# Attention and scan kernel: v projected straight into key rows, a second projection in place of the first chunk's swap, and a new order of the attention steps

## What is computed

```python
def _attn(a, sin, cos, ga, ba, gb, bb, Wq, Wkv, Wo, bo):
    an = _ln(a, ga, ba)
    bn = _ln(a, gb, bb)
    q = an @ Wq
    k, v = jnp.split(bn @ Wkv, 2, axis=-1)
    ...                                # 4 heads of 16 channels
    q = _rope(q, sin, cos)
    k = _rope(k, sin, cos)
    dots = jnp.einsum('bhid,bhjd->bhij', q, k)
    attn = jax.nn.softmax(dots, axis=-1)
    out = jnp.einsum('bhij,bhjd->bhid', attn, v)
    ...
    return jax.nn.elu(out @ Wo + bo)
...
xi = _attn(rows of x, ..._i);  xj = _attn(columns of x, ..._j)
return x + (xi + xj) / 2
```

## Time and profile before

| | us |
|---|---|
| median of 3 runs | 334.65 (333.85 to 337.41) |
| profiled execution | 336.71 |
| its span in the trace | 334.6 |
| TensorE busy | 235.9 (70%) |
| VectorE busy | 203.9 (61%) |
| ScalarE busy | 171.3 (51%) |
| GpSimd busy | 126.9 (38%) |

### The profile page before, as it was taken

One profiled execution on the slowest core, in us unless ns is written; L12 is line 12 of the kernel. 1 busy time (PEld: TensorE's weight loads), 2 busy tenths in 40 slices (PEclk: granted clock), 3 DMA queues, 4 the chain that ended last, 5 costly groups with the idle time before them and its releaser, 6 DMA issues.

```text
span 334.6 us, 7775 instructions
## 1 busy us (share of the span) xinstructions
PE 235.9 (70%) x3138; PEld 142.4 (43%) x3138; DVE 203.9 (61%) x333; ACT 171.3 (51%) x298; POOL 126.9 (38%) x104
## 2 busy tenths in 40 slices
PE   0366776886749694674259669998999867976453
PEld 0143444554425453452248335653444434445312
DVE  2668668684635453347535495899786868285333
ACT  2142554577553737183533674367447644933282
POOL 1411669114615160550040087367496971400000
PEclk9999798999996969597556989999799997997758
DMA  7510010433030303410354300000000000002002
GB/s 191 207 63 33 33 66 32 109 84 82 16 96 0 90 10 64 94 36 0 73 112 91 75 18 0 2 5 3 0 4 2 0 2 2 0 3 65 0 1 63
DMA packets 34243, 15.26 MB, mean 46 GB/s; under 512 B 31008, under 2 KB 31520, under 8 KB 34080
## 3 DMA queue, kind: packets, MB, share of 16 engines
q1 hardware_dynamic: 32480, 13.67, 16.1%
q10 hardware_dynamic: 1728, 1.10, 1.2%
HBM read 5.42 MB, written 2.10 MB: 22 GB/s over the span
## 4 chain that ended last, share of the span: by engine, by line
PE 38%; DVE 22%; ACT 17%; issue 11%; DMA 5%; SPq 5%; POOL 1%; ACTq 1%; DVEq 0%; POOLq 0%
PE ring L565 17%; PE score L565 8%; PE oz L565 4%; DMA rot_swap<-rot_sin 4%; PE ring L570 3%; PE p_turn L565 3%; SPq L537 3%; SPq L524 2%; DVE ln_v L864 2%; PE p_turn L570 2%; DVE mix L1142 2%; DVE ln_s L844 2%; ACT prob_t L1302 2%; DVE xhat L879 2%; DVE rot_sin L1006 2%
## 5 line engine op out<-in xcount | busy, mean ns | idle before, releaser
L1527 POOL TENSOR_TENSOR a_msk<-dt_fin,c_sb 128x512 f32<-128x512 f32 x32 | 39.7, 1239 | 34.4 <-DVE dt_fin L981 22.6
L1302 ACT ACTIVATE prob_t<-p_turn 128x512 f32<-128x512 f32 x32 | 17.7, 595 | 41.9 <-PE p_turn L570 41.8
L565 PE MATMUL score<-k_bd,q_rot 32*64 32x128 f32 x512 | 23.0, 330 | 17.6 <-POOL q_rot L895 16.0
L1142 DVE TENSOR_TENSOR mix<-dec,g_m 128x512 f32<-128x512 f32 x32 | 31.4, 987 | 2.2 <-ACT dec L1384 1.5
L1047 DVE TENSOR_REDUCE s_max<-score 128x16 f32<-128x1024 f32 x16 | 19.5, 1221 | 20.7 <-PE score L565 20.7
L1006 DVE SCALAR_TENSOR_TENSOR rot_cos<-ring,b_att,p_sb 128x512 f32<-128x512 f32 x15 | 11.2, 747 | 30.2 <-PE ring L565 17.2
L570 PE MATMUL ring<-c_sb,xhat 128*128 128x128 f32 x44 | 11.1, 401 | 25.1 <-DVE xhat L879 21.3
L565 PEld LDWEIGHTS score<-k_bd,q_rot 32*64 32x64 f32 x512 | 18.2, 165 | 23.5 <-POOL q_rot L895 18.2
L565 PE MATMUL score<-a_msk,c_sb 128*128 128x512 f32 x44 | 25.2, 656 | 0.0
L895 POOL TENSOR_TENSOR q_rot<-rot_cos,rot_swap 128x512 f32<-128x512 f32 x7 | 8.9, 1266 | 42.3 <-DMA rot_swap<-rot_sin 42.3
L1512 POOL TENSOR_TENSOR dtx<-xv,dt_fin 64x512 f32<-64x512 f32 x16 | 19.8, 1239 | 13.2 <-PE p_turn L565 12.2
(11 more groups left out here) (177 smaller groups left out, 582.6 us busy)
## 6 DMA issues: line engine op xcount, KB each, us to landing
...
```

The costliest lines, as they stand in the source:

```text
L565: return pe.matmul(dst, lhsT, rhs, start=start, stop=stop, skip_group_check=True)
L1142: v.tensor_tensor(mix[:, e % LAPS, :, :], dec[:, e % LAPS, :, :], wide(g_m[:, e // 4 % 2, e % 4, :], SSM_H), ALU.mult)\
L1302: a.activation(prob_t[:, e % 2, 4 * hp:4 * hp + 4, :].rearrange("p k n -> p (k n)"), PT[hp], ACT.Identity)\
L1527: gp.tensor_tensor(a_msk[:, m % LAPS, :, :], deep(dt_fin[:, 0, SSM_H * m:SSM_H * (m + 1)], GRID), wide(cst("tri"), SSM_H), ALU.mult).then_ ...
```

## The change

- **v.** Before, v was projected with channels as rows, drained with its bias by ScalarE (`v_sb`), turned by four transposes (`vt`) and copied to `v_bd` in two instructions. Now the normalised input is the stationary operand and the weight the moving one, so that v comes out with keys as rows: 8 products in the first pass, 32 in the second. ScalarE copies it straight to `v_bd`. The bias of v is folded into the output bias by two products (`bo`, in step 3).
- **Chunk 0.** k and q are projected a second time with swapped columns, onto the outer halves of the banks; the second multiplication of the rotation reads these, and no swap transfer is made. Both masks of k come from ScalarE, `k_rot` from VectorE. k(1) is projected before the first step, onto a `p_turn` bank.
- **Order of steps.** Before: even steps `wo`, `v`, `k` and `yt`, odd steps `vt` and `q`. Now: even steps `q` of the next chunk in slot b, `v` and `yt` in slot c; odd steps `wo` in a and `k` in b. Each q is projected one step later than before, each k one step later too.
- **ScalarE** executes the exponential before the slots a and b.
- **SyncE** issues both swaps of a second-pass chunk before the stores of a turned one.
- The normalising of tiles 1 to 3 is spread otherwise; the weight preparations move from ahead of steps 3 and 5 to the ends of steps 7 and 9, with `fold` in step 8.
- The parameter array grows by 128 columns in the first transfer and by 256 in the second.

```diff
-FOLD_STEP = 4
+FOLD_STEP = 8
+WEIGHTS = (dict(q=0, qs=1, k=2, ks=3, v=4), dict(q=0, k=1, v=2))
+BIASES = (0, 5)
...
-    steps = {-1: ([("xr", 0), ("k", 0), ("q", 0), ("xr", 1), ("v", 0), ("vt", 0)], [], [])}
+    steps = {-1: ([("xr", 0), ("k", 0), ("q", 0), ("v", 0), ("xr", 1), ("k", 1)], [], [])}
     for n in range(ATT_STEPS):
         g, odd = divmod(n, 2)
-        if n == 0:
-            a, b, c = [("k", 1)], [], []
-        elif n == 1:
-            a, b, c = [("xr", 2), ("q", 1)], [("v", 1)], [("k", 2), ("xr", 3)]
+        if n == 1:
+            a, b, c = [], [], [("xr", 2), ("k", 2)]
         elif n == 2:
-            a, b, c = [("vt", 1), ("q", 2)], [("v", 2)], [("k", 3)]
+            a, b, c = [], [("q", 2)], [("v", 1), ("xr", 3)]
+        elif n == 3:
+            a, b, c = [], [("k", 3)], [("bo", 0)]
         elif odd:
-            a, b, c = [("vt", g + 1)], [("q", g + 2)], []
+            a, b, c = [("wo", g - 2)] if g - 2 < ATT_CHUNKS - 1 else [], [("k", g + 2)], []
         else:
-            a, b, c = [("wo", g - 2)], [("v", g + 1)], [("k", g + 2), ("yt", g - 3)]
+            a, b, c = [("wo", g - 2)] if g - 2 == ATT_CHUNKS - 1 else [], [("q", g + 1)], [("v", g), ("yt", g - 3)] if n else []
...
-        if use == ("q", 0):
+        if use in (("q", 0), ("k", 1)):
...
+                sp.wait_ge((k_added, q_ready)[slot], g)
...
-            for g in range(CHUNKS):
+            for g in range(1, CHUNKS):
...
+                swap(CHUNKS + g, 1)
                 sp.wait_ge(y_turned, g + 1)
                 for a in range(2):
                     for m in range(2):
                         sp.dma_start(turned_w[a, m, g],
                                      y_tok[64 * a:64 * a + 64, g, :].rearrange("p (k m c) -> p k m c", k=4, m=2)[:, :, m, :])\
                             .then_inc(turned_out, 16)
-                swap(CHUNKS + g, 1)
...
+                if kind in ("q", "k"):
                     for r in range(2):
                         for a in range(2):
-                            last = mm(half_of(use, r)[64 * a:64 * a + 64, :], w_att[d][64 * r:64 * r + 64, at:at + DIM],
+                            last = mm(half_of(use, r)[64 * a:64 * a + 64, :], weight(w_att[d][64 * r:64 * r + 64, :], d, kind),
                                       xn_cols(d, c, r, a))
+                    if g == 0:
+                        for r in range(2):
+                            for a in range(2):
+                                last = mm(outer_half(use, r)[64 * a:64 * a + 64, :],
+                                          weight(w_att[d][64 * r:64 * r + 64, :], d, kind + "s"), xn_cols(d, c, r, a))
+                elif kind == "v" and d == 0:
+                    for k in range(2):
+                        for a in range(2):
+                            for u in range(2):
+                                last = mm(half_of(use, u)[:, DIM * (2 * k + a):DIM * (2 * k + a) + DIM],
+                                          xn_cols(0, c, u, a)[:, P * k:P * k + P], weight(w_att[d][64 * u:64 * u + 64, :], d, "v"))
+                elif kind == "v":
+                    for u in range(2):
+                        for k in range(2):
+                            for a in range(2):
+                                for m in range(2):
+                                    for r in range(2):
+                                        row = 64 * m + 32 * r
+                                        last = mm(half_of(use, u)[row:row + 32, DIM * (2 * k + a):DIM * (2 * k + a) + DIM],
+                                                  xn_i[64 * r:64 * r + 64, 16 * c + 8 * u + 4 * k + 2 * a + m, :],
+                                                  weight(w_att[d][64 * r:64 * r + 64, :], d, "v"))
...
-                elif kind == "vt":
-                    pe.wait_ge(v_copied, g + 1)
-                    last = turn(dst, v_sb[:, :])
+                elif kind == "bo":
+                    pe.wait_ge(mid_in, 16)
+                    pe.wait_ge(bias_here, 2)
+                    for d in range(2):
+                        at = BIASES[d] + WEIGHTS[d]["v"]
+                        last = mm(dst[:, d:d + 1], par("wo_" + "ji"[d]), b_att[:, at:at + 1])
...
+                    if e == 0:
+                        drained(pe, ("k", 1))
...
-            ln_mean(v, 1)
             ln_vector_b(v, 0)
-            ln_centre(v, 1)
             ln_vector_c(v, 0)
             v.wait_ge(bias_made, 1)
-            v.tensor_copy(b_att[:, 0:3], oz[:, 0:3]).then_inc(bias_here, 1)
+            v.tensor_copy(b_att[:, 0:4], oz[:, 0:4]).then_inc(bias_here, 1)
+            v.wait_ge(xa_in[1], 32)
+            ln_vector_a(v, 1)
+            ln_vector_b(v, 1)
...
+                    if g >= 1:
+                        v.scalar_tensor_tensor(rot_sin[:, slot, :].rearrange("p (t j) -> p t j", j=GRID),
+                                               middle(use).rearrange("p (t j) -> p t j", j=GRID), bias, table_of(d, sin_s[d][:, 0:(GRID, CW)[d]]),
                                                ALU.add, ALU.mult).then_inc(rotated, 1)
+                    else:
+                        v.scalar_tensor_tensor(rot_swap[:, slot, :].rearrange("p (r n) -> p r n", r=2), outer(use),
+                                               bias_at(d, kind + "s"),
+                                               wide(sin_s[0][:, :], 2),
+                                               ALU.add, ALU.mult).then_inc(rotated, 1)
+                elif kind == "bo":
+                    src = filled(v, use)
+                    for d in range(2):
+                        v.tensor_tensor(bo_v[:, d:d + 1], src[:, d:d + 1], col("bo_" + "ji"[d]), ALU.add).then_inc(bo_ready, 1)
...
+                if use == ("k", 0):
+                    k_sum(v, 0)
+                    ln_vector_c(v, 1)
                 if use == ("q", 0):
-                    ln_vector_b(v, 1)
-                    ln_vector_c(v, 1)
-                    v.wait_ge(xa_in[2], 32)
-                    ln_vector_a(v, 2)
-                    k_sum(v, 0)
-                    v.wait_ge(k_added, 1)
-                    k_mask(v, 0, 1)
                     q_sum(v, 0)
-                    v.wait_ge(bias_made, 2)
-                    v.tensor_copy(b_att[:, 3:6], oz[:, 3:6]).then_inc(bias_here, 1)
+            v.wait_ge(bias_made, 2)
+            v.tensor_copy(b_att[:, 4:8], oz[:, 4:8]).then_inc(bias_here, 1)
...
-                if n == FOLD_STEP - 1:
-                    late_weights()
-                if n == FOLD_STEP + 1:
-                    late_scales()
...
-                    ln_vector_b(v, 3)
+                    ln_vector_c(v, 2)
+                    v.wait_ge(xa_in[3], 32)
+                    ln_vector_a(v, 3)
                 for use in att_steps[n]:
                     if use[0] in ("k", "q"):
                         att_use(use)
-                    if use == ("q", 1):
-                        ln_vector_c(v, 3)
                 if n == 0:
+                    v.wait_ge(xa_in[2], 32)
+                    ln_vector_a(v, 2)
                     ln_vector_b(v, 2)
-                    ln_vector_c(v, 2)
-                    v.wait_ge(xa_in[3], 32)
-                    ln_vector_a(v, 3)
+                if n == 2:
+                    ln_vector_b(v, 3)
+                    ln_vector_c(v, 3)
                 g, odd = divmod(n, 2)
-                if odd and 0 <= g - 2 < ATT_CHUNKS:
-                    c = g - 2
+                c = g - 2
+                if (0 <= c < ATT_CHUNKS - 1) if odd else c == ATT_CHUNKS - 1:
                     v.wait_ge(wo_biased, c + 1)
                     v.scalar_tensor_tensor(y_t[:, c // CHUNKS, c % CHUNKS, :], wo_e[:, :], 1.0, wo_b[:, :], ALU.min, ALU.add)\
                         .then_inc(y_ready, 1)
                 for use in att_steps[n]:
                     if use[0] not in ("k", "q"):
                         att_use(use)
+                if n == FOLD_STEP - 1:
+                    late_weights()
+                if n == FOLD_STEP + 1:
+                    late_scales()
...
-                    d = g // CHUNKS
-                    if g >= 1:
-                        filled(a, ("vt", g - 1))
-                    a.wait_ge(bias_here, 1 + d)
-                    a.activation(in_order(d, v_sb[:, :]), as_made(d, middle(use)), ACT.Identity,
-                                 bias=b_att[:, 3 * d + 2:3 * d + 3]).then_inc(v_copied, 1)
-                elif kind == "vt":
-                    src = filled(a, use)
...
-                        a.activation(v_bd[rows, g % 2, :, HD * m:HD * m + HD], src[rows, :].rearrange("p (t d) -> p t d", d=HD),
+                        a.activation(v_bd[rows, g % 2, :, HD * m:HD * m + HD], middle(use)[rows, :].rearrange("p (t d) -> p t d", d=HD),
...
-                    a.activation(k_bd[:, 0, 0, :], k_rot[:, :], ACT.Identity, scale=cst("head_mask")[:, 0:1]).then_inc(k_ready, 1)
-                att_use(use)
+                    for r in range(2):
```

(7 more changed lines are left out.)

109 lines of the change are left out of this document (68 added, 41 removed).

## The result

| | before | after |
|---|---|---|
| median (4 runs each) | 335.07 us | 322.11 us |
| lowest to highest | 333.85 to 337.41 | 317.66 to 322.88 |
| profiled execution, span | 336.71, 334.6 | 321.89, 319.8 |
| ratio of runs, 95% interval | | 0.956 [0.945, 0.968] |

The forecast was 317.5 (310 to 325), with 0.92 for faster. The mechanisms happened as described, and most of the laps came within 1 us.

The account below looks back on a forecast made before the run. Attention was taken as bound by q standing in SyncE's queue behind the stores. -19.8 + 1.3 + 0.9 = -17.6 took the profiled 336.71 to 319.1, 317.0 for runs; 0.5 for small waits gave 317.5 us (310 to 325).

Parts of the forecast that it names:

- Front: Start up to scores 4: first scores at 20.8 us instead of 23.79, scores of step 4 at 49.0 against 56.66.
- the removed transfers cover the second projections: Before the first scores: k and q cost 1.1 us more each, but chunk 0's swap transfers and their waits go.
- Step 4 to 6: From scores 4 to scores 6: a lap of 10.3 us, without a late y_t in step 3.
- Step 7: Step 7's s_cen ends 12.6 us later than step 5's 59.2, at 71.8.
- Step 8: x_tok loads and weight block arrive late together: scores start at 76.3 us, block decides by 0.3, s_max at 77.7.
- 8 to 10: Lap from step 8 to 10: 13.2 us against 15.8, with the fold holding step 9's scores to 86.7.
- The laps from 10: Steps 10 to 14: two laps of 13.0 us plus 1.0 for the scales; scores 14 at 116.6 against 136.35.
- y_t's wait: Odd second-pass steps: y_t waits for ScalarE's drain behind the exponential, from 1.35 to 2.45 us after s_cen's end.
- v behind q's rotation: Second pass: v waits for q's rotation, 7.0 us after odd s_cen's end, takes 1.3; next scores queue behind it.
- q hidden by 0.7 at the least: Second pass: with its swap issued before the stores, q_rot is hidden by at least 0.7 us.
- The rival by which v is dear: Second pass: v's 64 instructions cost far more than 20 ns each; 328 us at 62 ns, 362 at 195; chance 0.04.
- Tail: Scores 14 to x_tok: the 15.7 us of before plus 1.3 for chunk 5's drain; 0.9 more for the second x_tok.

Follow-up runs that it names:

- a_dma0: The changed kernel with chunk 0's swap made by transfers again, without the second projection's eight products: 318.0 us, ratio 0.951.
- a_fold5: The changed kernel with weight block, fold and scales three steps earlier (block behind step 4, fold in step 5): 314.9 us, ratio 0.935.
- a_act: The changed kernel with ScalarE's old order, the output product drained ahead of the exponential of the same odd step: 316.7 us, ratio 0.944.
- a_act_v: The changed kernel with ScalarE's old order (drains ahead of the exponential) and v projected ahead of q's projection: 317.5 us, ratio 0.945.
- b_sp: The kernel before with only SyncE's order changed, both swaps of a second-pass chunk ahead of the four stores: 312.8 us, ratio 0.933.

## Why the prediction was right, and where it was not

- **Front.** Scores 0 at 20.8, measured 21.16; step 2: 36.0, 36.48; step 3: 45.0, 45.59; step 4: 49.0, 50.07. Right within 1.1. v's 8 products (16 instructions) were taken as 1.8 and took 1.97 at the lower level; the biases 1.53 in place of 0.8. The statement that the removed transfers cover the second projections was tested by itself (a_dma0) and holds.
- **Step 4 to 6.** 10.3, measured 11.1. v of the first pass at 1.11 and 1.37, not 0.9.
- **Step 7.** Its s_cen was to end at 71.8 and ends at 74.3: 1.0 of that was there at step 5, and 1.5 came in steps 6 and 7, where the granted clock stood at 0.50 from 68 to 70 us.
- **Step 8.** Scores at 76.3, measured 77.85, released by q_rot; the block was to decide by 0.3, and it does decide, by far more: w_ops starts at 78.27 and s_max at 81.32, in place of 77.7. Of these 3.6, 2.5 are step 7's late s_cen and 0.9 are y_t, which took 1.60 there in place of 0.69.
- **8 to 10 is the step that failed in size**: 13.2 forecast, 16.0 measured, the largest single miss. Scores 8, set by the loads, were only 1.6 late, but s_max behind the block was 3.6 late, so 2.1 more lie between the two than I had. From that s_max to scores 9 it takes 7.7, with 0.88 idle on TensorE for o_t, 1.27 for q's rotation and 1.36 for the drain of y, near my 7.9. The other 0.9 lie behind step 9's s_cen: I had scores 10 start 0.1 after its end, and they start 1.0 after it. And block, fold and scales cost 7 us where they stand, as a_fold5 shows, where my sum had them nearly hidden behind the loads. They did not only lie beside the loads' stall: they held s_max and o_t, and with them the products behind.
- **The laps from 10.** 14.0 and 13.1 for 10 to 12 and 12 to 14, measured 14.4 and 12.7. The two holds in them were named: y_t's wait at 1.05 (measured 0.95 to 1.10, and 1.3 per lap by a_act), and v behind q's rotation (0.9 and 0.4 by the laps of a_act and a_act_v from 10 to 12 and 12 to 14).
- **q hidden by 0.7 at the least**: right, q_rot ends 4.6, 3.6 and 1.5 ahead of the scores of steps 10, 12 and 14 (at 89.2 for scores at 93.84). One row was misread on the way: the transfer at 97.69 stands behind two more issues at 96.36 and ends after q_rot's start at 99.04, so it is the swap of the next k and not q's. The 4.0 from q's first issue to q_rot, which the cover goes by, are right.
- **v's 64 instructions at 1.3**: 1.10, 17 ns each, and once 1.68. The rival by which v is dear is out.
- **Tail.** 17.0 from scores 14 to x_tok, 16.8 measured. Behind x_tok it takes 182.0; I had 183.4, the 182.5 of before and 0.9.

So the sum was 4.4 short at scores 14 (15.35 gained against 19.8), 1.6 of it built up by scores 8 and 2.8 in the lap from 8 to 10. Of the 4.4, 0.2 and 1.4 came back in the tail, so that the profiled execution is 2.8 above the 319.1 of the sum. The 1.4 are luck: the same program behind x_tok differs by 6 from profile to profile. The 4.6 of the medians have another part that no mechanism stands for: I had put the median 2.06 below the profiled time, as before, and for the changed kernel it lies 0.2 above it (2.8 and 2.3, less the 0.5 that I had added for small waits).

What the prediction did not ask, because it only compared the new order with the old, is how much of the gain the new order of steps is the reason for. It listed y_t's wait and v's place as costs, and had it summed a lap without them, it would have come near the 11.3 that b_sp runs at: 13.0 less 1.05 and less what v's place adds. The 16.0 of idle time ended by q_rot in the profile of before would have said the same.
